# Squares of the context in a distance matrix: by ScalarE and in the bank's emptying, in place of a matmul pair, with the stage's order rewritten

## The chip, the cores and the metric

The kernel runs on 1 core of one Trainium2 chip. The metric is the device time of one execution in microseconds (us); lower is better.

## What is computed

A decoder of two layers over 64 batches of 256 tokens of width 256, with a context of 77 rows of width 256 for each batch, all in float32. Each sublayer is followed by a layer norm. What matters here is the second layer: self-attention (16 heads, rotary), and then an alignment of the context with the tokens by dynamic time warping, which begins with a matrix of Euclidean distances.

```python
def _pairwise_euclidean(a, b):
    aa = jnp.sum(a * a, axis=-1)[:, None]
    bb = jnp.sum(b * b, axis=-1)[None, :]
    ab = a @ b.T
    return jnp.sqrt(jnp.maximum(aa + bb - 2.0 * ab, 0.0))
```

Here `a` is the context (77 rows) and `b` the tokens after the layer norm (256 rows).

## The kernel before

The program has four stages, A to D, each a pass over all 64 batches, with the tokens stored to memory between them. A is self-attention of layer 0, B its cross-attention and feed-forward, C the rotary self-attention of layer 1 and the distances, D the expansion along the warping path and the last attention. Between C and D, a separate block takes the square roots and runs the warping itself.

Within a stage, a batch is a chain of steps, each named by its kind. `ORDER` gives for every engine a list of numbers, 100 x lag + place in the chain; round r of an engine's line runs, for each entry, that place of the chain for batch r - lag. So the order on each engine is written out by hand, five batches are in flight, and only semaphores tie the engines together. Adding one number of rounds to all lags of an engine changes nothing. What matters is the cyclic order of the entries and their lags relative to each other.

The steps of stage C that the text speaks of, by the names used below, with their lines on TensorE:

- "q", "k", "v": projections of the tokens, eight records each (L782 with `A_wq`, `A_wk`, `A_wv`); "oproj" is the output projection (L782 with `A_wo`). Four matmuls in float32 leave eight records, two for each.
- "max 0" to "max 3": bf16 scores from which VectorE takes row maxima (L881; VectorE L1206). "shift 0" and "shift 1" turn these maxima (L892; VectorE L1213).
- "core 0" to "core 3": scores in float32 with 32 rows of the array for each head (L814, 16 records; ScalarE's exponentials L1020, four for each core step).
- "pv 0", "pv 1": values weighted by probabilities, in 32 columns for each head (L834, 32 records). "norm" turns the result (L904).
- "xT C": turns the tokens loaded for a new batch (L792 with `Cx`); it waits for that load (SyncE, L736). "xT A3" turns the finished tokens for the distances.
- "ln": layer norm (VectorE L1270 and L1274, GpSimd L1134 to L1141). "rot": rotary on keys by VectorE (L700 to L703) and on queries by GpSimd.
- "dist": the distances. GpSimd squares the turned tokens and the turned context (L1153 to L1156, the second into `csq`, a view of the key buffer `kb`); TensorE accumulates four matmul pairs (L962); VectorE empties the bank (L1314).

The eight PSUM banks go round: each use of a bank waits until the use eight before it was emptied. SyncE has one queue in the order store of distances, load of tokens for the batch five later, fetch of the context turned, store of tokens; the load thus stands behind the wait for `dist_ready`.

The four matmuls of a distance step before:

```python
for i, (lhs, rhs) in enumerate(((ctxT[s][:, 0, :], xT[s][:, 0, :]), (ctxT[s][:, 1, :], xT[s][:, 1, :]),
                                (neg_half[:, 0:C], xsq[s][:, 0, :]), (csq[s][:, 0, :], neg_half[:]))):
    ins = pe.matmul(ck.bank(step)[0:C, 0:S], lhs, rhs, start=(i == 0), stop=(i == 3))
```

Of the kernel before, what the change touches and what calls it, by code (L numbers as in the profile page):

```python
# [33 lines left out]
S = 256  # L34
C = 77
# [139 lines left out]
def chain(phase, b):  # L175
# [10 lines left out]
    else:  # L186
# [42 lines left out]
    },  # L229
    "C": {  # L230
        "pe": (
            525, 415, 202, 307, 629, 416, 308, 203, 309, 526, 204, 417, 310, 418, 420, 312, 630, 313, 421,
            314, 423, 424, 101, 206,
        ),
        "act": (
            425, 207, 529, 317, 319, 320, 212, 322, 214, 1, 106,
        ),
        "dve": (
            204, 527, 205, 630, 313, 423, 424, 315, 102, 316, 208, 103, 209, 426, 210,
        ),  # L240
        "pool": (
            530, 323, 427, 5,
        ),
        "sp": (
            631, 100, 311, 528,
        ),
    },
    "D": {
# [45 lines left out]
def signals(step, engine):  # L294

    kind, att = step[0], step[1]
    return {
        "pe": {"core": ["scores_ready"] * 4, "pv": ["weighted"]},
        "act": {
            "q": ["q_rounded", "q_ready"] * (att in ("A1", "A2")), "qT": ["q_rounded", "q_ready"],  # L300
            "k": ["k_rounded", "k_ready"] * (att != "A3"), "kT": ["k_rounded", "k_ready"],
            "core": ["probs_ready"] * 4, "take": ["out_taken"], "xT": ["xT_ready"], "oT": ["attnT_ready"],
            "xqT": ["xqT_ready"], "gu": ["tanh_ready"], "hq": ["hid_rounded", "hq_ready"], "hT": ["hqT_ready"],
            "mix": ["exps_ready"], "v": ["v_ready"] * (att in VALUES_BY_ACT),
        },
        "dve": {
            "q": ["q_tokens"] * (att in ("A3", "A4")), "k": ["q_tokens"] * (att == "A3"), "v": ["v_ready"] * (att not in VALUES_BY_ACT),
            "rot": ["dve_step", "k_rotated"] if att == "A3" else ["norms2"],
            "max": ["max_done"] * ROW_GROUPS.get(att, 0), "shift": ["q_shifted"] * 2,
            "norm": ["dve_step", "normed"] + ["x_used"] * (att == "A1" and step[-1] == 1),  # L310
            "oproj": ["proj_taken"], "path": ["dve_step", "path_ready"], "expand": ["x4_used"],
            "down": ["down_taken"], "ln": ["dve_step", "var_ready"], "fq": ["dve_step"] * 3 + ["scales_ready"],
            "gu": ["gated", "hid_ready"], "hq": ["dve_step"] * 3 + ["scale_ready"], "dist": ["dist_ready"],
            "gate": ["logits_taken", "logits_ready"], "mix": ["dve_step"] * 5 + ["mixed"],
        },
        "pool": {
            "sq": ["squared"], "rot": ["pool_step", "rotated"] if att == "A3" else ["pool_step"] * 3 + ["rotated"],
            "xT": ["base_ready"] * (att == "B"),
            "norm": ["base_ready"] * (att in ("A3", "A4") and step[-1] == 0),
            "fq": ["pool_step", "xq_ready"], "ln": ["pool_step", "pool_step", "x_ready"], "dist": ["pool_step", "squares_ready"],  # L320
        },
        "sp": {},
    }[engine].get(kind, [])
# [61 lines left out]
def build(nc, nb, io, out):  # L385
    stack = ExitStack()
    with stack:
# [138 lines left out]
        class Tiles:  # L526


            def __init__(self, phase, where):
# [56 lines left out]
                if phase == "C":  # L586
                    self.xT, self.x = each("xT", [P, FC, S]), self.at
                    self.ctxT, self.dist = each("ctxT", [P, FC, C]), each("dist", [C, S])
                    self.csq = [t[:, 0:FC * C].rearrange("p (c n) -> p c n", c=FC) for t in self.kb_f]
                    self.xsq, self.r2, self.r3 = self.qe[0], self.res, self.ke[0]  # L590
                if phase == "D":
                    self.xT = self.atT
# [10 lines left out]
        def segment(phase, tiles, lines, counts, base, where):  # L603
# [14 lines left out]
            if phase in "CD":  # L618
                qk, qr = tiles.qk, tiles.qr
            if phase == "C":  # L620
                ctxT, csq, xsq, dist, r2, r3 = tiles.ctxT, tiles.csq, tiles.xsq, tiles.dist, tiles.r2, tiles.r3
            if phase == "D":
                path, ctx, ends, sq, nrm = tiles.path, tiles.ctx, tiles.ends, tiles.sq, tiles.nrm
                lg, ex, top, gs = tiles.lg, tiles.ex, tiles.top, tiles.gs
# [82 lines left out]
            def _(sp):  # L707
                def one(dram, b):

                    part = dram[b:b + 1] if isinstance(b, int) else dram[bass.ds(b, 1)]  # L710
                    return part.rearrange("o p n -> p o n")

                def do(ck, step):
# [23 lines left out]
                    elif kind == "fetch" and what == "A":  # L737
                        ck.wait_earlier("x_used", ("norm", "A1", b, 1))
                        sp.dma_start(x0[s][:].rearrange("p a b -> p (a b)").unsqueeze(1),
                                     one(io["x"], b)).then_inc(x_loaded[s], 16)  # L740
                    elif kind == "fetch":
                        ck.wait_earlier("dist_ready", ("dist", "A3", b))
                        sp.dma_start(ctxT[s][:].rearrange("p a b -> p (a b)").unsqueeze(1),
                                     one(io["ctxT"], b)).then_inc(ctx_loaded[s], 16)
                    elif what == "D":
                        ck.wait("dist_ready", ("dist", "A3", b))
                        sp.dma_start(one(dist_dram, b), dist[s][:].unsqueeze(1)).then_inc(dist_stored[s], 16)
                    else:
                        ck.wait("x_ready", ("ln", what, b))
                        sp.dma_start(one(x_dram[phase], b),  # L750
                                     x[s][:].rearrange("p a b -> p (a b)").unsqueeze(1)).then_inc(
                                         tokens_stored[phase][s], 16)
# [9 lines left out]
            def _(pe):  # L762
# [75 lines left out]
                def do(ck, step):  # L838
# [115 lines left out]
                    elif kind == "dist":  # L954

                        ck.wait("xT_ready", ("xT", att, b))
                        pe.wait_ge(ctx_loaded[s], 16 * (ck.turn + 1))
                        ck.wait("squares_ready", step)
                        ck.wait_bank_free(step)
                        for i, (lhs, rhs) in enumerate(((ctxT[s][:, 0, :], xT[s][:, 0, :]), (ctxT[s][:, 1, :], xT[s][:, 1, :]),  # L960
                                                        (neg_half[:, 0:C], xsq[s][:, 0, :]), (csq[s][:, 0, :], neg_half[:]))):
                            ins = pe.matmul(ck.bank(step)[0:C, 0:S], lhs, rhs, start=(i == 0), stop=(i == 3))  # L962
                        ck.filled(ins, step)
                    elif kind == "expand":
                        ck.wait("path_ready", ("path", "E", b))
# [19 lines left out]
            def _(act):  # L985
# [20 lines left out]
                def do(ck, step):  # L1006
# [59 lines left out]
                    elif kind == "hT":  # L1066
                        t = step[3]
                        ck.wait_bank_full(step)
                        ins = act.activation(hqT[s][:, t].rearrange("p a b -> p (a b)"),
                                             ck.bank(step)[:].bitcast(BF16), ACT.Copy)  # L1070
                        ck.tell(ins, "hqT_ready", step)
                    elif kind == "mix":
                        ck.wait("logits_ready", ("gate", att, b))
                        for t in range(QT):
                            for i, (low, high) in enumerate(((0, H - 1), (H - 1, H + 1))):
                                ins = act.activation(ex[s][:, t, low:high], lg[s][:, t, low:high], ACT.Exp,
                                                     bias=gs[s][:, i, t:t + 1], accum_out=gs[s][:, 2 + i, t:t + 1])
                        ck.tell(ins, "exps_ready", step)
                    else:
                        return  # L1080
# [5 lines left out]
            def _(pool):  # L1086
# [3 lines left out]
                def do(ck, step):  # L1090
# [58 lines left out]
                        ck.tell(pool.tensor_scalar(xq[s][:], xq_f[s][:], MAGIC, QMAX, ALU.subtract, ALU.min), "xq_ready", step)  # L1149
                    elif kind == "dist":  # L1150
                        ck.wait("xT_ready", ("xT", att, b))
                        pool.wait_ge(ctx_loaded[s], 16 * (ck.turn + 1))
                        pool.tensor_tensor(xsq[s][:], xT[s][:], xT[s][:], ALU.mult)  # L1153
                        link(ck, pool.tensor_tensor(csq[s][:], ctxT[s][:], ctxT[s][:], ALU.mult))
                        pool.tensor_tensor(xsq[s][:, 0, :], xsq[s][:, 0, :], xsq[s][:, 1, :], ALU.add)
                        ck.tell(pool.tensor_tensor(csq[s][:, 0, :], csq[s][:, 0, :], csq[s][:, 1, :], ALU.add),  # L1156
                                "squares_ready", step)

                walk(pool, "pool", do)
# [3 lines left out]
            def _(dve):  # L1163
# [3 lines left out]
                def do(ck, step):  # L1167
# [142 lines left out]
                        ck.wait("scale_ready", step)  # L1310
                    elif kind == "dist":
                        ck.wait_bank_full(step)
                        ck.stored(dist_stored[s])
                        ins = dve.tensor_scalar(dist[s][:], ck.bank(step)[0:C, 0:S], -2.0, 0.0, ALU.mult, ALU.max)  # L1314
                        ck.tell(ins, "dist_ready", step)
                    elif kind == "gate":
                        ck.wait_bank_full(step)
# [96 lines left out]
        with ExitStack() as where:  # L1414
# [29 lines left out]
            def _(act):  # L1444
                def root(t):
                    if t % PART == 0:
                        act.wait_ge(dist_loaded[t // PART % 2], 32 * (t // PART // 2 + 1))
                    act.activation(cost[:, t + 1, 1:W + 1], cost[:, t + 1, 1:W + 1], ACT.Sqrt).then_inc(roots_ready, 1)

                for t in range(PART):  # L1450
                    root(t)
# [129 lines left out]
```

## Time and profile before

| what | value |
|---|---|
| times of 3 runs | 5856.48, 5843.52, 5859.08 us; median 5856.48 |
| the profiled execution | 5858.39 us, its span 5856.6 us |
| TensorE busy over the span | 5289.1 us (90%) |
| VectorE busy | 4889.5 us (83%) |
| ScalarE busy | 4166.3 us (71%) |
| GpSimd busy | 2753.9 us (47%) |
| mean granted TensorE clock | 0.964 |

Stage C runs from about 2650 to 4170 us of the span. The engines' shares are means over four stages with different limits, so the rows that count are those of stage C. The 1.8 us between the execution's time and its span lie around the first and the last instruction.

### The profile page before, as it was taken

Reading aid. Unit: us, or ns where it says so; the run is one execution under the profiler, and the core shown is the slowest. Engines: PE = TensorE matmul, PEld = TensorE weight load, DVE = VectorE, ACT = ScalarE, POOL = GpSimd, SP = SyncE. Lnnn points to the kernel's source line nnn. Section 1 sums busy time; section 2 is a strip of 40 time slices with the busy share of each in tenths; the row PEclk is TensorE's granted clock in tenths of the full one; section 3 lists DMA queues with packets and bytes.
Section 4 is the critical chain, followed back from the end, with each engine's and each line's share of the span. In section 5 each row is a group of like instructions: output and inputs, shape, how many; then the busy total and the mean of one; then the engine's idle time right before and its main releaser. Section 6 shows DMA issues by size and latency. Waiting matters only on the chain. (4 is left out here: it accounts for less than half of the span.)

```text
span 5856.6 us, 138862 instructions
## 1 busy us (share of the span) xinstructions
PE 5289.1 (90%) x54914; PEld 3660.6 (63%) x54914; DVE 4889.5 (83%) x11487; ACT 4166.3 (71%) x7921; POOL 2753.9 (47%) x2766
## 2 busy tenths in 40 slices
PE   6999999969999999987999999999308999999998
PEld 4666666646666666655666666666206667666666
DVE  6888888859999999986878778778677888888887
ACT  5777777748888888875666666666326777777776
POOL 0122111125555555543545545545106777777775
PEclk9999999989999999999999999999659999999999
DMA  1111111111111111001010010010110001101000
GB/s 55 45 45 45 48 45 46 45 36 30 30 30 30 31 30 29 30 23 35 30 34 30 30 34 30 30 34 30 38 30 14 31 26 31 31 26 31 28 29 23
DMA packets 140516, 194.01 MB, mean 33 GB/s; under 512 B 26080, under 2 KB 63840, under 8 KB 139488
## 3 DMA queue, kind: packets, MB, share of 16 engines
q1 hardware_dynamic: 139872, 185.13, 10.1%
q8 instruction: 440, 7.21, 0.5%
q14 instruction: 204, 1.67, 0.1%
HBM read 112.90 MB, written 72.18 MB: 32 GB/s over the span
## 5 line engine op out<-in xcount | busy, mean ns | idle before, releaser
L1020 ACT ACTIVATE Cpr<-pj 128x512 f32<-128x512 f32 x1024 | 522.2, 614 | 426.9 <-PE pj L814 426.9
L1206 DVE TENSOR_REDUCE Amp<-pj 128x2 f32<-128x512 f32 x1024 | 629.5, 682 | 97.8 <-PE pj L881 97.8
L1206 DVE TENSOR_REDUCE Cmp<-pj 128x2 f32<-128x512 f32 x1024 | 634.4, 682 | 77.7 <-PE pj L881 77.7
L1020 ACT ACTIVATE Apr<-pj 128x512 f32<-128x512 f32 x1024 | 522.1, 613 | 172.7 <-PE pj L814 172.7
L1206 DVE TENSOR_REDUCE Dmp<-pj 128x2 f32<-128x512 f32 x1024 | 633.2, 681 | 6.1 <-PE pj L881 6.1
L1020 ACT ACTIVATE Dpr<-pj 128x512 f32<-128x512 f32 x1024 | 520.2, 610 | 101.1 <-PE pj L814 101.0
L1134 POOL TENSOR_SCALAR Ave<-Amv 128x2 f32<-128x2 f32 x64 | 14.6, 228 | 971.7 <-DVE Amv L1274 971.7
L1106 POOL TENSOR_TENSOR Dnrm<-Dnrm,power 128x32 f32<-128x32 f32 x64 | 348.8, 5449 | 122.7 <-DVE Dnrm L1184 122.7
L700 POOL TENSOR_TENSOR Cqr<-Cqk,rope_cos 128x512 f32<-128x512 f32 x64 | 81.6, 1274 | 564.0 <-DVE Cqk L1174 564.0
L1141 POOL TENSOR_SCALAR Dx<-Dres,Dmv,Drstd 128x256 f32<-128x256 f32 x256 | 312.3, 1230 | 28.9 <-POOL Drstd L1135 28.9
L1141 POOL TENSOR_SCALAR Bx<-Bres,Bmv,Brstd 128x256 f32<-128x256 f32 x256 | 311.9, 1225 | 29.6 <-POOL Brstd L1135 29.6
L814 PE MATMUL pj<-Aq,Ak 32*128 32x256 f32 x4096 | 291.5, 391 | 2.1 <-DVE Aq L1213 1.2
L814 PE MATMUL pj<-Dq,Dk 32*128 32x256 f32 x4096 | 281.9, 398 | 0.4 <-ACT Dpr L1020 0.2
L814 PE MATMUL pj<-Cq,Ck 32*128 32x256 f32 x4096 | 277.9, 395 | 1.0 <-DVE Cq L1213 0.6
L1134 POOL TENSOR_SCALAR Bve<-Bmv 128x2 f32<-128x2 f32 x128 | 29.2, 228 | 501.7 <-DVE Bmv L1274 501.7
L1020 ACT ACTIVATE Bpr<-pj 77x512 f32<-77x512 f32 x512 | 261.0, 590 | 5.1 <-PE pj L814 5.1
L968 PE MATMUL pj<-Dctx,Dkb 77*128 77x256 f32 x256 | 67.9, 388 | 210.8 <-DVE Dkb L1246 210.8
L834 PE MATMUL pj<-Dpr,Dv 128*32 128x256 f32 x4096 | 250.3, 385 | 0.2 <-ACT Dpr L1020 0.2
L834 PE MATMUL pj<-Apr,Av 128*32 128x256 f32 x4096 | 247.6, 382 | 1.3 <-ACT Apr L1020 1.1
L834 PE MATMUL pj<-Cpr,Cv 128*32 128x256 f32 x4096 | 247.6, 382 | 0.3 <-ACT Cpr L1020 0.3
L814 PEld LDWEIGHTS pj<-Cq,Ck 32*128 32x128 f32 x4096 | 193.1, 185 | 82.9 <-issue 52.4
L814 PEld LDWEIGHTS pj<-Dq,Dk 32*128 32x128 f32 x4096 | 196.5, 186 | 76.6 <-issue 67.8
(305 smaller groups left out, 15111.7 us busy)
## 6 DMA issues: line engine op xcount, KB each, us to landing
Ax0T<-in_xT SPq DMA_DIRECT2D x64, 256.0 KB, 3.0
Ax<-in_x SPq DMA_DIRECT2D x64, 256.0 KB, 3.0
x_A_scratch<-Ax SPq DMA_DIRECT2D x64, 256.0 KB, 2.1
Bx<-x_A_scratch SPq DMA_DIRECT2D x64, 256.0 KB, 2.9
x_B_scratch<-Bx SPq DMA_DIRECT2D x64, 256.0 KB, 2.0
Cx<-x_B_scratch SPq DMA_DIRECT2D x64, 256.0 KB, 3.1
x_C_scratch<-Cqr SPq DMA_DIRECT2D x64, 256.0 KB, 3.0
Dx<-x_C_scratch SPq DMA_DIRECT2D x64, 256.0 KB
```

The source lines that it names most:

```text
L700: eng.tensor_tensor(dst, src, cos, ALU.mult)
L814: ins = pe.matmul(ck.bank(step + (bank,))[0:n, at:at + S], ke[e][s][p0:p0 + 32, c, k:k + n], qe[e][s][p0:p0 + 32, c, :], start=True, stop= ...
L834: ins = pe.matmul(ck.bank(step)[r:r + VW, at:at + S], vv[s][0:n, i, h, :], probs, start=(i == 0), stop=(i == len(tiles_) - 1), skip_group_ ...
L968: ins = pe.matmul(ck.bank(step)[:, t * D:(t + 1) * D], path[s][:, t * P:(t + 1) * P], ctx[s][:], start=True, stop=True)
L1020: ck.tell(act.activation(dst, ck.bank(step + (bank,))[0:n, :], ACT.Exp, scale=HD ** -0.5), "probs_ready", step)
L1106: link(ck, pool.tensor_tensor(nrm[s][:, 1].rearrange("p t h -> p (t h)"), nrm[s][:, 0].rearrange("p t h -> p (t h)"), power[:], ALU.pow))
L1134: link(ck, pool.tensor_scalar(ve[s][:, :, 0:1], mv[s][:, :, 1:2], EPS, None, ALU.add))
L1141: ins = pool.tensor_scalar(x[s][:, t], res[s][:, t], mv[s][:, t, 0:1], rstd[s][:, t, 0:1], ALU.subtract, ALU.mult)
L1206: ins = dve.tensor_reduce(dst, src, AX.X, ALU.max, negate=True)
```

## The change

The squares of the context leave the matmul sum. SyncE fetches the context untransposed into `dist` (77 x 256) right behind the turned one. A new ScalarE step squares it in place with a sum along the row (`accum_out`) and halves the sum into `ctx_norm`. TensorE then runs three pairs, and GpSimd only squares the tokens. VectorE empties the bank by subtracting `ctx_norm` and taking the minimum with 0; the factor -2 moves into the scale of the square root. VectorE's step no longer waits for the store of five batches before, since the new fetch does.

```diff
@@ SyncE, fetch
                         sp.dma_start(ctxT[s][:].rearrange("p a b -> p (a b)").unsqueeze(1),
                                      one(io["ctxT"], b)).then_inc(ctx_loaded[s], 16)
+                        ck.stored(dist_stored[s])
+                        sp.dma_start(dist[s][:].unsqueeze(1), one(io["ctx"], b)).then_inc(ctx_loaded[s], 16)
@@ TensorE, dist
-                        pe.wait_ge(ctx_loaded[s], 16 * (ck.turn + 1))
+                        pe.wait_ge(ctx_loaded[s], 32 * (ck.turn + 1))
-                                                        (neg_half[:, 0:C], xsq[s][:, 0, :]), (csq[s][:, 0, :], neg_half[:]))):
-                            ins = pe.matmul(ck.bank(step)[0:C, 0:S], lhs, rhs, start=(i == 0), stop=(i == 3))
+                                                        (neg_half[:, 0:C], xsq[s][:, 0, :]))):
+                            ins = pe.matmul(ck.bank(step)[0:C, 0:S], lhs, rhs, start=(i == 0), stop=(i == 2))
@@ ScalarE
+                    elif kind == "dist":
+                        act.wait_ge(ctx_loaded[s], 32 * (ck.turn + 1))
+                        ck.tell(act.activation(dist[s][:], dist[s][:], ACT.Square, accum_out=ctx_norm[s][:, 0:1]), "ctx_squared", step)
+                        ck.wait("ctx_squared", step)
+                        ck.tell(act.activation(ctx_norm[s][:, 1:2], ctx_norm[s][:, 0:1], ACT.Copy, scale=0.5), "ctx_normed", step)
@@ GpSimd, dist
-                        pool.tensor_tensor(xsq[s][:], xT[s][:], xT[s][:], ALU.mult)
-                        link(ck, pool.tensor_tensor(csq[s][:], ctxT[s][:], ctxT[s][:], ALU.mult))
-                        pool.tensor_tensor(xsq[s][:, 0, :], xsq[s][:, 0, :], xsq[s][:, 1, :], ALU.add)
-                        ck.tell(pool.tensor_tensor(csq[s][:, 0, :], csq[s][:, 0, :], csq[s][:, 1, :], ALU.add),
+                        link(ck, pool.tensor_tensor(xsq[s][:], xT[s][:], xT[s][:], ALU.mult))
+                        ck.tell(pool.tensor_tensor(xsq[s][:, 0, :], xsq[s][:, 0, :], xsq[s][:, 1, :], ALU.add),
                                 "squares_ready", step)
@@ VectorE, dist
-                        ck.stored(dist_stored[s])
-                        ins = dve.tensor_scalar(dist[s][:], ck.bank(step)[0:C, 0:S], -2.0, 0.0, ALU.mult, ALU.max)
+                        ck.wait("ctx_normed", step)
+                        ins = dve.tensor_scalar(dist[s][:], ck.bank(step)[0:C, 0:S], ctx_norm[s][:, 1:2], 0.0, ALU.subtract, ALU.min)
@@ square roots, ahead of the warping
-                    act.activation(cost[:, t + 1, 1:W + 1], cost[:, t + 1, 1:W + 1], ACT.Sqrt).then_inc(roots_ready, 1)
+                    act.activation(cost[:, t + 1, 1:W + 1], cost[:, t + 1, 1:W + 1], ACT.Sqrt, scale=-2.0).then_inc(roots_ready, 1)
@@ ORDER["C"], the numbers of pool and sp (pe, act and dve are rewritten too)
-            530, 323, 427, 5,
+            523, 727, 730, 305,
-            631, 100, 311, 528,
+            200, 511, 628, 631,
```

The table for stage C is rewritten for all engines. Freed of the common number of rounds, it changes four things. On TensorE, "oproj" and "core 2" move ahead of "k", and "v" moves behind "shift 0"; all other neighbours, and all lags, stay. VectorE follows with "oproj" ahead of "k" and "v" behind "ln". GpSimd runs "dist" right behind "ln" of the same batch and ahead of the next "rot", and adds the bias for the output projection one round earlier. SyncE fetches the context one round later.

TensorE, from "max 0" to the first rows of "pv 0" in a round of stage C, before (`A_wk` is k, `A_wo` is oproj, `A_wv` is v; L814 is core 2, L892 shift 0):

```order
L881 MATMUL pj<-Ckb,Cqb_2 128x256 x8
L782 MATMUL pj<-A_wk,CxT 128x256 x4
L881 MATMUL pj<-Ckb,Cqb_2 128x256 x8
L782 MATMUL pj<-A_wo,Cqr 128x256 x4
L782 MATMUL pj<-A_wv,CxT 128x256 x4
L814 MATMUL pj<-Cq,Ck_1 128x256 x8
L892 MATMUL pj<-ident,Cmp 128x128 x2
L834 MATMUL pj<-Cpr_0,Cv 32x256 x2
```

The same place after the change, up to where "pv 0" begins (each line number is larger by 2):

```order
L883 MATMUL pj<-Ckb,Cqb_2 128x256 x8
L784 MATMUL pj<-A_wo,Cqr 128x256 x4
L816 MATMUL pj<-Cq,Ck_1 128x256 x8
L784 MATMUL pj<-A_wk,CxT 128x256 x4
L883 MATMUL pj<-Ckb,Cqb_2 128x256 x8
L836 MATMUL pj<-Cpr_0,Cv 32x256 x2
```

Two projections in a row became two with a step of 32-row scores between them, and "max 1" now stands directly ahead of "pv 0".

TensorE, from the end of "pv 0" to "max 2", before (the first L814 is core 3, the second core 0; L962 is dist):

```order
L834 MATMUL pj<-Cpr_3,Cv 32x256 x2
L814 MATMUL pj<-Cq,Ck_1 128x256 x8
L814 MATMUL pj<-Cq,Ck_2 128x256 x8
L962 MATMUL pj<-CxT,CctxT 77x256 x2
L962 MATMUL pj<-Cq,neg_half 77x256
L962 MATMUL pj<-neg_half,Ckb 77x256
L881 MATMUL pj<-Ckb,Cqb_2 128x256 x8
```

The same place after:

```order
L836 MATMUL pj<-Cpr_3,Cv 32x256 x2
L816 MATMUL pj<-Cq,Ck_1 128x256 x8
L894 MATMUL pj<-ident,Cmp 128x128 x2
L784 MATMUL pj<-A_wv,CxT 128x256 x4
L816 MATMUL pj<-Cq,Ck_2 128x256 x8
L964 MATMUL pj<-CxT,CctxT 77x256 x2
L964 MATMUL pj<-Cq,neg_half 77x256
L883 MATMUL pj<-Ckb,Cqb_2 128x256 x8
```

Core 3 and core 0 stood side by side and now have "shift 0" and "v" between them; the pair with `Ckb` (the context's squares) is gone.

ScalarE after the change, from the end of the exponentials of core 3 to the start of those of core 0:

```order
L1022 ACTIVATE Cpr_3<-pj 128x512
L1076 ACTIVATE Cdist,Cctx_norm<-Cdist 77x256
L1078 ACTIVATE Cctx_norm<-Cctx_norm 77x1
L1022 ACTIVATE Cpr_0<-pj 128x512
L1022 ACTIVATE Cpr_1<-pj 128x512
```

Before, the exponentials of core 0 followed those of core 3 with nothing between.

## Rows read from the trace of the kernel before

**Rows 1.** Windows: 200 us of stage C; PE, PEld, DVE, ACT, POOL, clock, DMA share, GB/s.

```profile
3400.00:3600.00 200.00, 196.97 (x2022) 136.74 (x2018) 159.25 (x324) 128.74 (x240) 103.66 (x117) 1.00 0.10 30
```

**Rows 2.** Waits, 2800 to 4000 us (52 rounds): total us, times, longest us.

```profile
PEld pj L792 <- DMA Cx<-x_B_scratch: 9.5, 15, 1.1
```

**Rows 3.** Timeline of TensorE in one round: start, us, line, tiles, records, idle before.

```profile
3399.99 1.99 PE L782 MATMUL pj<-A_wk,CxT 128*128 128x256 f32 x8
3401.91 0.40 PE L881 MATMUL pj<-Ckb,Cqb 32*128 32x256 bf16 x8
3402.24 1.99 PE L782 MATMUL pj<-A_wo,Cqr 128*128 128x256 f32 x8
3404.07 1.89 PE L782 MATMUL pj<-A_wv,CxT 128*128 128x256 f32 x8
3405.89 1.15 PE L814 MATMUL pj<-Cq,Ck 32*128 32x256 f32 x16
3406.97 0.44 PE L892 MATMUL pj<-ident,Cmp 128*128 128x128 f32 x2
3407.33 1.93 PE L834 MATMUL pj<-Cpr,Cv 128*32 128x256 f32 x32
3409.20 2.01 PE L814 MATMUL pj<-Cq,Ck 32*128 32x256 f32 x32
3411.14 1.09 PE L962 MATMUL pj<-CxT,CctxT 128*77 128x256 f32 x4
3412.06 0.59 PE L962 MATMUL pj<-Cq,neg_half 128*77 128x256 f32 x2
3412.49 0.59 PE L962 MATMUL pj<-neg_half,Ckb 128*77 128x256 f32 x2
3413.06 0.40 PE L881 MATMUL pj<-Ckb,Cqb 32*128 32x256 bf16 x8
3413.46 1.93 PE L834 MATMUL pj<-Cpr,Cv 128*32 128x256 f32 x32
3415.32 1.15 PE L814 MATMUL pj<-Cq,Ck 32*128 32x256 f32 x16
3416.40 1.09 PE L904 MATMUL pj<-ident,Cqk 128*128 128x128 f32 x8
3417.70 0.66 PE L792 MATMUL pj<-ident,Cx 128*128 128x128 f32 x4 [0.21 <-DMA Cx<-x_B_scratch]
3418.19 1.04 PE L792 MATMUL pj<-ident,Cqr 128*128 128x128 f32 x8
```

**Rows 4.** Timeline of VectorE in the same round.

```profile
3403.35 2.47 DVE L1206 TENSOR_REDUCE Cmp<-pj 128x2 f32<-128x512 f32 x4
...
3408.24 0.68 DVE L1196 TENSOR_TENSOR Cv<-pj,A_bv 128x512 f32<-128x512 f32 x1
...
3413.13 0.42 DVE L1314 TENSOR_SCALAR Cdist<-pj 77x256 f32<-77x256 f32 x1 [1.18 <-PE pj L962]
```

**Rows 5.** Timeline of SyncE's queue in the same round: the load of tokens.

```profile
3413.93 0.34 SPq L736 DMA_DIRECT2D Cx<-x_B_scratch  x1
```

**Rows 6.** The page, section 6: that load's median us from issue to landing.

```profile
Cx<-x_B_scratch SPq DMA_DIRECT2D x64, 256.0 KB, 3.1
```

**Rows 7.** Timeline of ScalarE in the same round: exponentials of core 3 and core 0.

```profile
3410.36 4.03 ACT L1020 ACTIVATE Cpr<-pj 128x512 f32<-128x512 f32 x8 [0.43 <-PE pj L814]
```

**Rows 8.** ScalarE in stage D: ns min/median/max, first and last start, forms.

```profile
L1036 ACT ACTIVATE Dqr<-pj,A_bv_col x128: 467/470/475, 4456.0 to 5842.2; 128x256 f32<-128x256 f32 x128
L1076 ACT ACTIVATION_READ_ACCUMULATOR Dex<-Dlg,Dgs x256: 185/191/194, 4461.9 to 5845.7; 128x1 f32 x128
```

**Rows 9.** Timeline of stage A: a GpSimd step and a VectorE step beside it.

```profile
599.62 2.58 POOL L1141 TENSOR_SCALAR Ax<-Aat,Amv,Arstd 128x256 f32<-128x256 f32 x2 [0.24 <-POOL Arstd L1135]
...
600.41 0.69 DVE L1229 TENSOR_TENSOR Aat<-Ax,Aat 128x512 f32<-128x512 f32 x1
```

**Rows 10.** A VectorE line of stage D with two inputs in SBUF (columns as rows 8).

```profile
L1337 DVE SCALAR_TENSOR_TENSOR Dgs<-Dex,Dgs x128: 146/158/1265, 4466.5 to 5846.7; 128x2 f32<-128x2 f32 x128
```

More of the change, by code:

```diff
@@ L231 @@
         "pe": (
-            525, 415, 202, 307, 629, 416, 308, 203, 309, 526, 204, 417, 310, 418, 420, 312, 630, 313, 421,
-            314, 423, 424, 101, 206,
+            321, 214, 323, 324, 1, 106, 325, 215, 2, 107, 429, 216, 108, 326, 217, 3, 109, 218, 220, 110, 4,
+            112, 430, 113,
         ),
         "act": (
-            425, 207, 529, 317, 319, 320, 212, 322, 214, 1, 106,
+            317, 319, 320, 530, 212, 322, 214, 1, 106, 325, 107, 429,
         ),
         "dve": (
-            204, 527, 205, 630, 313, 423, 424, 315, 102, 316, 208, 103, 209, 426, 210,
+            210, 427, 104, 105, 530, 213, 323, 324, 215, 2, 216, 108, 326, 3, 109,
         ),
         "pool": (
-            530, 323, 427, 5,
+            523, 727, 730, 305,
         ),
         "sp": (
-            631, 100, 311, 528,
+            200, 511, 628, 631,
         ),
@@ L303, in signals @@
             "xqT": ["xqT_ready"], "gu": ["tanh_ready"], "hq": ["hid_rounded", "hq_ready"], "hT": ["hqT_ready"],
-            "mix": ["exps_ready"], "v": ["v_ready"] * (att in VALUES_BY_ACT),
+            "dist": ["ctx_squared", "ctx_normed"], "mix": ["exps_ready"], "v": ["v_ready"] * (att in VALUES_BY_ACT),
         },
@@ L588, in __init__ @@
                     self.ctxT, self.dist = each("ctxT", [P, FC, C]), each("dist", [C, S])
-                    self.csq = [t[:, 0:FC * C].rearrange("p (c n) -> p c n", c=FC) for t in self.kb_f]
+                    self.ctx_norm = each("ctx_norm", [C, 2])
                     self.xsq, self.r2, self.r3 = self.qe[0], self.res, self.ke[0]
@@ L620, in segment @@
             if phase == "C":
-                ctxT, csq, xsq, dist, r2, r3 = tiles.ctxT, tiles.csq, tiles.xsq, tiles.dist, tiles.r2, tiles.r3
+                ctxT, ctx_norm, xsq, dist, r2, r3 = tiles.ctxT, tiles.ctx_norm, tiles.xsq, tiles.dist, tiles.r2, tiles.r3
             if phase == "D":
@@ L1151, in do @@
                         ck.wait("xT_ready", ("xT", att, b))
-                        pool.wait_ge(ctx_loaded[s], 16 * (ck.turn + 1))
-                        pool.tensor_tensor(xsq[s][:], xT[s][:], xT[s][:], ALU.mult)
-                        link(ck, pool.tensor_tensor(csq[s][:], ctxT[s][:], ctxT[s][:], ALU.mult))
-                        pool.tensor_tensor(xsq[s][:, 0, :], xsq[s][:, 0, :], xsq[s][:, 1, :], ALU.add)
-                        ck.tell(pool.tensor_tensor(csq[s][:, 0, :], csq[s][:, 0, :], csq[s][:, 1, :], ALU.add),
+                        link(ck, pool.tensor_tensor(xsq[s][:], xT[s][:], xT[s][:], ALU.mult))
+                        ck.tell(pool.tensor_tensor(xsq[s][:, 0, :], xsq[s][:, 0, :], xsq[s][:, 1, :], ALU.add),
                                 "squares_ready", step)
```

## The prediction

> **What bounds it now.** I went by stages. The page's busy shares are means over four stages, so the windows come first. In a stretch of stage C TensorE is busy 197 of 200 us at a granted clock of 1.00, which is the 2.4 GHz level; VectorE has 159, ScalarE 129, GpSimd 104 [rows 1]. TensorE bounds this stage. The waits then show where it still stands still: 15 times in 52 rounds its turning of new tokens ("xT C") stood until their load landed, 9.5 us in all and 1.1 at most [rows 2]. Last I read one round on all queues [rows 3 to 5, 7]. The distances' emptying by VectorE waited 1.18 us for TensorE [rows 4], and ScalarE's exponentials 0.43 [rows 7]: the other engines follow TensorE. A saving there counts in full, if its own cost and that load don't take it back.
>
> **The removed pair.** Between the pair with `neg_half` as weights and the pair with `Ckb` lie 0.43 us (3412.06 to 3412.49) [rows 3]. One pair less per batch is 64 x 0.43 = 27.6 us less. All of it is on the path.
>
> **The rewritten order on TensorE.** Here I price each block from its start to the start of the next, and ask what stood on both sides of it. "k", between two kinds of 32-row steps, took 1.92 (3399.99 to 3401.91). "oproj", entered from such a step and left to a projection, took 1.83, and "v", entered from a projection and left to a 32-row step, 1.82. So each border costs some 0.09 to 0.1. "Core 1", alone between "pv 1" and "norm", took 1.08, and so did "core 2". Core 3 and core 0 side by side took 1.94 (3409.20 to 3411.14), 0.22 less than two alone. "Max 1" before a projection took 0.33, "max 2" before "pv 1" 0.40 [rows 3]. In the new order:
> - core 3 and core 0 stand apart: 2.16 in place of 1.94, +0.22;
> - "oproj" now has 32-row steps on both sides: 1.92 in place of 1.83, +0.09; "k" had and has them, "v" still leaves to one and is entered from full-width work: 0 each;
> - "max 1" runs into "pv 0": 0.40 in place of 0.33, +0.07;
> - "shift 0" (0.36) is left to "v" and no longer to "pv 0": one border less, -0.09.
>
> The sum is +0.29 per round, 64 x 0.29 = 18.6 us. So the new order gives back two thirds of the pair. The trace has each of these neighbourhoods except the shift into a projection; if that were free or cost a border more, the sum would be 0.2 or 0.38, 13 or 24 us.
>
> The Trainium skill has this as a rule that speaks against the change: "TensorEngine Tiling (Array Packing)", section "Key Properties", says that changing the tiling mode drains the engine. By that rule alone, without a size, the order costs something; the rows agree, with their 0.09 to 0.22 a border.
>
> **The load behind the distances.** SyncE issues the load only after `dist_ready`. In this round it was issued at 3413.93, its median time to landing is 3.1, so it lands at 3417.03 [rows 5, 6]. TensorE could have turned it at about 3417.33: "norm" begins at 3416.40 and eight transposes take 0.93 (four take 0.49, 3417.70 to 3418.19) [rows 3]. The median margin is 0.3. What does the change do to it? Before, VectorE worked 3.71 us on "v", "ln" and "rot" (from 3408.24 until 1.18 before 3413.13) [rows 4] and was done early. Its "v" began 1.27 after "shift 0" on TensorE (3406.97) [rows 3]. After, VectorE's 1.27 + 3.71 = 4.98 after "shift 0" stand against TensorE's 0.27 ("shift 0") + 1.82 ("v") + 1.08 (core 0) + 1.49 (three pairs, from 1.92 less 0.43) + 0.03 = 4.69. So VectorE empties the distances 0.29 later than TensorE would let it, and the load loses 0.29 of its margin. The 15 rounds that wait already wait 0.29 longer, 4.4 us; of the 37 others about a quarter have less margin than that and wait half of it on average, 1 to 2 us. For 64 rounds that makes some 6 us [rows 2]. Bounds: 0 if VectorE is never late, and 64 x 0.29 = 18.6 if every round waited.
>
> **What I cost at nothing.** ScalarE's new work is a square over 77 x 256, an accumulator read and a copy of one column. The nearest rows are 0.47 for 128 x 256 from PSUM and 0.19 for the read [rows 8]; with a copy of about 0.3 (less than the 0.47) it is some 1.0 us. The cover: the eight exponentials of core 3 and core 0 began 1.16 after TensorE's start of core 3 and took 4.03 together [rows 3, 7]. Core 0 now starts 0.27 + 1.82 + 1.08 = 3.17 after core 3, while four exponentials need 2.0, so 1.16 us lie open between them. Were it to take longer, the first to wait is core 0's first bank, needed by "max 2" 2.57 after core 0 starts and free after 1.16 + 0.5: another 0.9 of room. ScalarE's wait for the fetch is a full round and more behind its landing.
>
> VectorE must end "max 1" before "shift 0": TensorE leaves 0.40 + 1.86 + 1.08 = 3.34 between their starts; VectorE needs the emptying of "k" (0.6, as the like 0.68 shape less overlap) and 2.47 for the four maxima [rows 3, 4], 3.2 with two hand-overs. That fits by 0.1; were it to miss by 0.1, 6 us come on top. GpSimd drops two of its four squares, which were off the path except for the very last batch, where they save under 1 us. "dist" on GpSimd now waits for the tokens turned in the next round ahead of "rot", whose result is needed only at that round's end. The extra fetch (77 KB a batch) is queued behind the load. VectorE's and the root's new scalars keep the shapes. Stages A, B and D don't change.
>
> **The sum.** -27.6 + 18.6 + 6 = -3.0 us. The profiled execution took 5858.4 (its span 5856.6 and 1.8 around it), which gives 5855. It lies 1.9 above the median of the runs, 5856.5, on which I set the forecast: 5853.
>
> **Rivals.**
> - *The whole pair is gained* (5829, faster). The borders cost nothing net, or the order lets something else run sooner, and the load stays hidden: -27.6. For it: TensorE is the bound at 197 of 200 us, and 37 rounds of 52 don't wait for the load. Against it: the 1.94 against 2.16 for two core steps is plain in one round. Chance 0.18.
> - *The load lands late* (slower). The new fetch and the store share the engines with the load, or VectorE's "rot" is late. The margin is 0.3, and beyond it each 0.1 costs up to 6.4 us. At 0.6 more than forecast nearly all rounds wait 0.5, +32 us, 5882; it decides from about 0.4 more. For it: the waits of up to 1.1 [rows 2] show that landings scatter by more than the margin. Against: the fetch is queued behind. Chance 0.11.
> - *GpSimd holds VectorE up* (slower). "Rot" has two inputs in SBUF and now falls beside GpSimd's layer norm (two instructions of 1.2 to 1.3). A two-element step of the same sort took 1.265 at most where 0.158 is its median [rows 10]. One such hold of 1.2 in each round would cost about 1.2 x 64 = 77 less what margin is left: 5915. Against: in stage A the same layer norm step (600 us) ran beside a VectorE step with two such inputs, which took 0.69 [rows 9], no more than a step of 128 x 512 in stage C, 0.68 [rows 4]. The Trainium skill, "GPSIMD Engine Reference", section "Key points", names this contention for VectorE instructions with two SBUF inputs. By that rule the hold would come; the trace disagrees for this pair of instructions [rows 9] and agrees for another [rows 10]. Chance 0.05.
> - My forecast, within 0.3%: 0.66.
>
> **How the numbers follow.** 0.3% is 17.6 us, about what a measurement of this kernel tells from no change. Forecast and its neighbours (order cost 13 to 24, load 0 to 18.6, a missed "shift 0" 6) span -15 to +15 and 5842 to 5868. The first rival is faster; a part of the forecast's own lower end adds to it: faster 0.20. Slower takes the second and third: 0.16. Same 0.64. The range reaches to 5831, nearly the full gain, and to 5876, where a late load begins to show.
>
> **What would show it.** In the new trace: three pairs of L964 with 0.43 less to "max 2"; core 3 and core 0 at 1.08 each, "oproj" at 1.92, "max 1" at 0.40; a round slightly under the 23.1 us of before (1200 us over 52 rounds). Waits of "xT C" for `Cx` in more rounds, 0.2 to 0.4 us longer. ScalarE's square and copy inside idle time, with no wait of VectorE's emptying on them. VectorE's emptying of the distances no longer idle before it. Wrong would be: a wait of "shift 0" for VectorE's maxima; VectorE's "rot" instructions longer beside GpSimd's layer norm; loads landing later than 3.1; or core steps apart that cost no more than together, which would give the whole pair.

## The result, and the profile after

The changed kernel took 5825.28 us in the median of 4 runs (5815.69 to 5825.86), the kernel before 5852.93 in the median of 4 beside it (5843.52 to 5859.08). The ratio is 0.995, with a 95% interval of 0.9938 to 0.9962: faster by 27.6 us. A second, later comparison (E5 below) gave 0.9954 (0.9941 to 0.9968). The forecast was 5853, at most down to 5831. So the prediction was wrong in size. The time is that of its first rival, "the whole pair is gained" (5829), but the runs below show another way to it. Two executions below, one of the ten of E2 (11572.56 us) and one of the 25 of the kernel before beside it (5965.34), ran at a lower granted clock (0.741 and 0.917, all others 0.964 to 0.967), and the ratios leave them out. The changed kernel's profiled execution took 5824.72 us.

The page of the changed kernel, sections 1 and 6: busy time, share and instructions of each engine; the token load with its median time to landing.

```profile
span 5822.9 us, 138676 instructions
PE 5262.6 (90%) x54786; PEld 3621.4 (62%) x54786; DVE 4894.9 (84%) x11487; ACT 4205.2 (72%) x8113; POOL 2746.1 (47%) x2638
...
Cx<-x_B_scratch SPq DMA_DIRECT2D x64, 256.0 KB, 3.0
```

TensorE lost 26.5 us of busy time, ScalarE gained 38.9. The 200 us of stage C that answer to [rows 1], in the windows of the changed kernel:

```profile
3400.00:3600.00 200.00, 197.23 (x2014) 135.22 (x2010) 160.88 (x326) 139.16 (x275) 99.46 (x97) 1.00 0.11 34
```

TensorE bounds the stage as before (197 of 200, at the same clock); ScalarE has 10 us more. Next, one round of TensorE, which answers to [rows 3]: the timeline, from "core 1" after "pv 1" to the next "pv 1".

```profile
3399.07 1.15 PE L816 MATMUL pj<-Cq,Ck 32*128 32x256 f32 x16
...
3406.37 0.40 PE L883 MATMUL pj<-Ckb,Cqb 32*128 32x256 bf16 x8
3406.70 1.99 PE L784 MATMUL pj<-A_wo,Cqr 128*128 128x256 f32 x8
3408.62 1.15 PE L816 MATMUL pj<-Cq,Ck 32*128 32x256 f32 x16
3409.70 1.99 PE L784 MATMUL pj<-A_wk,CxT 128*128 128x256 f32 x8
3411.62 0.40 PE L883 MATMUL pj<-Ckb,Cqb 32*128 32x256 bf16 x8
3411.95 1.93 PE L836 MATMUL pj<-Cpr,Cv 128*32 128x256 f32 x32
3413.81 1.15 PE L816 MATMUL pj<-Cq,Ck 32*128 32x256 f32 x16
3414.89 0.44 PE L894 MATMUL pj<-ident,Cmp 128*128 128x128 f32 x2
3415.16 1.89 PE L784 MATMUL pj<-A_wv,CxT 128*128 128x256 f32 x8
3416.99 1.15 PE L816 MATMUL pj<-Cq,Ck 32*128 32x256 f32 x16
3418.06 1.09 PE L964 MATMUL pj<-CxT,CctxT 128*77 128x256 f32 x4
3418.99 0.59 PE L964 MATMUL pj<-Cq,neg_half 128*77 128x256 f32 x2
3419.51 0.40 PE L883 MATMUL pj<-Ckb,Cqb 32*128 32x256 bf16 x8
3419.84 1.50 PE L836 MATMUL pj<-Cpr,Cv 128*32 128x256 f32 x24
```

From start to start: "oproj" 1.92 (forecast 1.92), core 3 (3413.81) and core 0 (3416.99) 1.08 and 1.07 (forecast 1.08 each), "shift 0" 0.27 (0.27). Two blocks differ from the forecast. "Max 1" before "pv 0" took 0.33 (3411.62 to 3411.95) and not 0.40; and "max 2" before "pv 1" now takes 0.33 as well, where it took 0.40 [rows 3]. The distances took 1.45 (3418.06 to 3419.51), 0.47 less than the 1.92 of before, though the pair is 0.43.

What TensorE's weights wait for at that place stands in the timeline of its weight loads. Before, from the distances to "pv 1":

```profile
3412.28 0.36 PEld L962 LDWEIGHTS pj<-neg_half,Ckb 128*77 128x77 f32 x2
3413.03 0.15 PEld L881 LDWEIGHTS pj<-Ckb,Cqb 32*128 32x128 bf16 x8 [0.39 <-ACT Cpr L1020]
3413.46 1.45 PEld L834 LDWEIGHTS pj<-Cpr,Cv 128*32 128x32 f32 x32 [0.28 <-ACT Cpr L1020]
```

The same in the changed kernel:

```profile
3418.77 0.36 PEld L964 LDWEIGHTS pj<-Cq,neg_half 128*77 128x77 f32 x2
3419.51 0.12 PEld L883 LDWEIGHTS pj<-Ckb,Cqb 32*128 32x128 bf16 x8 [0.37 <-ACT Cpr L1022]
3419.84 1.24 PEld L836 LDWEIGHTS pj<-Cpr,Cv 128*32 128x32 f32 x28 [0.21 <-ACT Cpr L1022]
```

The weight loads stand idle for a while here in every run; 0.37 and 0.21 are what the changed kernel and E2 below have in the mean of all rounds, 0.39 and 0.28 are more. So a wait of TensorE on ScalarE of 0.07 (and 0.02 to 0.04 ahead of "max 2") was in the trace of before, and the prediction did not use it. The releaser's name alone does not tell, since ScalarE is named in both kernels; the length does.

ScalarE in the same round, which answers to [rows 7]: timeline, with idle time before and its releaser.

```profile
3414.98 2.06 ACT L1022 ACTIVATE Cpr<-pj 128x512 f32<-128x512 f32 x4 [0.43 <-PE pj L816]
3416.90 0.42 ACT L1076 ACTIVATE Cdist<-Cdist 77x256 f32<-77x256 f32 x1
3417.20 0.21 ACT L1076 ACTIVATION_READ_ACCUMULATOR Cdist<-Cdist 77x1 f32 x1
3417.45 0.20 ACT L1078 ACTIVATE Cctx_norm<-Cctx_norm 77x1 f32<-77x1 f32 x1
3418.15 2.06 ACT L1022 ACTIVATE Cpr<-pj 128x512 f32<-128x512 f32 x4 [0.50 <-PE pj L816]
```

The eight exponentials that ran in one row are two fours now; the square, its read and the copy lie between them, 0.75 from 3416.90 to 3417.65, with 0.50 to spare. VectorE, which answers to [rows 4]:

```profile
3415.37 0.88 DVE L1217 SCALAR_TENSOR_TENSOR Cq<-pj,mask,Cq 128x256 f32<-128x256 f32 x2 [0.55 <-PE pj L894]
...
3419.18 0.69 DVE L703 TENSOR_TENSOR Cqr<-Cqr,Ck 128x512 f32<-128x512 f32 x1
3419.78 0.47 DVE L1318 TENSOR_SCALAR Cdist<-pj,Cctx_norm 77x256 f32<-77x256 f32 x1
```

VectorE waits for "shift 0" and not the reverse, though its maxima (L1210) end only 0.08 before "shift 0" begins on TensorE, near the 0.1 of the forecast. It comes to the distances without idle time, as forecast, and in the median begins emptying them 0.20 after TensorE's last pair ended, where it was 0.04 before. The waits of the changed kernel, 2800 to 4000 us (53 rounds), against [rows 2]:

```profile
PEld pj L794 <- DMA Cx<-x_B_scratch: 8.8, 17, 1.3
```

More rounds wait for the load (17 against 15), but in all no longer than before.

### The profile page after: what moved, and what is told of

Read it like the earlier page. It is cut to its first block and busy times, and to the rows that moved or that the text cites. A ratio compares the mean times of both kernels' runs of the same rounds, so it can differ in the third digit from the quotient of the medians.

```text
span 5822.9 us, 138676 instructions
## 1 busy us (share of the span) xinstructions
PE 5262.6 (90%) x54786; PEld 3621.4 (62%) x54786; DVE 4894.9 (84%) x11487; ACT 4205.2 (72%) x8113; POOL 2746.1 (47%) x2638
## 5 line engine op out<-in xcount | busy, mean ns | idle before, releaser
L1210 DVE TENSOR_REDUCE Amp<-pj 128x2 f32<-128x512 f32 x1024 | 630.0, 684 | 86.3 <-PE pj L883 86.3
L1210 DVE TENSOR_REDUCE Cmp<-pj 128x2 f32<-128x512 f32 x1024 | 634.2, 683 | 73.0 <-PE pj L883 73.0
L1210 DVE TENSOR_REDUCE Dmp<-pj 128x2 f32<-128x512 f32 x1024 | 633.8, 683 | 7.1 <-PE pj L883 7.1
L1159 POOL TENSOR_TENSOR Cq<-CxT 128x512 f32<-128x512 f32 x64 | 66.5, 1038 | 537.8 <-ACT CxT L1044 537.8
L816 PE MATMUL pj<-Cq,Ck 32*128 32x256 f32 x4096 | 295.3, 400 | 1.5 <-DVE Cq L1217 0.6
L1027 ACT ACTIVATE Cqk<-pj 128x512 f32<-128x512 f32 x128 | 76.5, 597 | 233.2 <-PE pj L836 233.2
```

The lines of the kernel that those rows point to most:

```text
L816: ins = pe.matmul(ck.bank(step + (bank,))[0:n, at:at + S], ke[e][s][p0:p0 + 32, c, k:k + n], qe[e][s][p0:p0 + 32, c, :], start=True, stop= ...
L1027: ins = act.activation(outT[s][:, 2 * octet:2 * octet + 2].rearrange("p a b -> p (a b)"), ck.bank(("pv", att, b, octet))[:], ACT.Copy)
L1159: link(ck, pool.tensor_tensor(xsq[s][:], xT[s][:], xT[s][:], ALU.mult))
L1210: ins = dve.tensor_reduce(dst, src, AX.X, ALU.max, negate=True)
```

## The experiments

Theory S (for stall): in the old order ScalarE's eight exponentials in a row hold up "max 2" and "pv 1". They began at 3410.36, one takes 0.61, and they come every 0.49 ((4.03 - 0.61) / 7). "Max 2" waits for its four banks before its first matmul, and the last of them is the one that the fifth exponential, the first of core 0, empties at 3410.36 + 4 x 0.49 + 0.61 = 3412.93; it began at 3413.06. "Pv 1" takes the bank of the sixth, free at 3413.42, and began at 3413.46 [rows 3, 7]. (In the trace these two exponentials end at 3412.92 and 3413.41.) If so, the pair alone gains nothing, because "max 2" can't come sooner; the new order alone costs its borders and gives the stall back; only both together gain. Rival B (for borders): the price of a border was misread, and pair and order each count for themselves. Rival L: the load's landings changed, because of the fetch or of GpSimd's order.

**E1: three pairs, order of before.** The changed kernel's computation, with the order of before on every engine.

```diff
         "pe": (
-            321, 214, 323, 324, 1, 106, 325, 215, 2, 107, 429, 216, 108, 326, 217, 3, 109, 218, 220, 110, 4,
-            112, 430, 113,
+            525, 415, 202, 307, 629, 416, 308, 203, 309, 526, 204, 417, 310, 418, 420, 312, 630, 313, 421,
+            314, 423, 424, 101, 206,
...
         "act": (
-            317, 319, 320, 530, 212, 322, 214, 1, 106, 325, 107, 429,
+            425, 207, 529, 530, 317, 319, 320, 212, 322, 214, 1, 106,
...
```

> The change's computation (three pairs, ScalarE's squares, GpSimd's two squares fewer) in the order of before; ScalarE's new step stands in its long idle time behind xT A3. Theory S (in the old order ScalarE's eight exponentials in a row hold max 2 and pv 1 back; the removed pair leaves TensorE only more time to wait for them): max 2 begins no earlier after core 3 than before (3.86 us), the round stays at 22.95 and the time at that of before, 5853, within 6 us. Rival P (the pair's time and some stall with it are a matter of the pair alone): the round shortens by 0.43 to 0.54 and the time is 5853 - 28 to - 34 = 5819 to 5825, that of the changed kernel.

Measured: 5849.32 (10 runs) against 5854.21 (25), ratio 0.9995 (0.9986 to 1.0005). The pair is out, and at most 8 us came of it, where its 0.43 a round would make 28. Its TensorE timeline shows where it went:

```profile
3407.36 2.01 PE L816 MATMUL pj<-Cq,Ck 32*128 32x256 f32 x32
3409.30 1.09 PE L964 MATMUL pj<-CxT,CctxT 128*77 128x256 f32 x4
3410.22 0.59 PE L964 MATMUL pj<-Cq,neg_half 128*77 128x256 f32 x2
3411.22 0.40 PE L883 MATMUL pj<-Ckb,Cqb 32*128 32x256 bf16 x8 [0.40 <-ACT Cpr L1022]
3411.62 1.93 PE L836 MATMUL pj<-Cpr,Cv 128*32 128x256 f32 x32
```

From core 3 to "max 2" it is 3.86, as before (3409.20 to 3413.06 [rows 3]). The 0.43 of the pair turned into a wait of 0.40 for ScalarE, whose eight exponentials began 1.16 after core 3, as in [rows 3, 7]. The round stayed at 22.955. All 52 rounds between 2800 and 4000 us have this wait. That is what S says; by B the round would be shorter by 0.43.

**E2: four pairs, new order.** The computation of before with the order of after (without ScalarE's new step).

```diff
         "pe": (
...
+            321, 214, 323, 324, 1, 106, 325, 215, 2, 107, 429, 216, 108, 326, 217, 3, 109, 218, 220, 110, 4,
+            112, 430, 113,
...
         "act": (
-            425, 207, 529, 317, 319, 320, 212, 322, 214, 1, 106,
+            317, 319, 320, 212, 322, 214, 1, 106, 325, 107, 429,
...
```

> The computation of before in the changed order, on all engines. Theory S: borders cost 0.21 (core 3 and core 0 apart), 0.09 (oproj) and -0.09 (shift 0), the two stalls of 0.04 and 0.07 behind dist and max 2 go: +0.10 a round, a round of 23.06 without a load wait, and 5853 + 6 = 5859. My forecast's pricing, in which 0.40 for max 2 was a border: +0.29 a round, 5871. Rival P: the order is neutral or a gain: 5853 or less.

Measured: 5857.15 (10 runs) against 5854.21, ratio 1.0005 (0.9995 to 1.0014); the round (the median spacing of VectorE's emptyings of the distances) 23.06, against 22.955 before. Its timeline, from core 0:

```profile
3407.90 1.15 PE L814 MATMUL pj<-Cq,Ck 32*128 32x256 f32 x16
3408.98 1.09 PE L962 MATMUL pj<-CxT,CctxT 128*77 128x256 f32 x4
...
3410.34 0.59 PE L962 MATMUL pj<-neg_half,Ckb 128*77 128x256 f32 x2
3410.86 0.40 PE L881 MATMUL pj<-Ckb,Cqb 32*128 32x256 bf16 x8
3411.19 1.07 PE L834 MATMUL pj<-Cpr,Cv 128*32 128x256 f32 x16
```

With all four pairs the distances take 1.88 and "max 2" 0.33: no stall. The borders cost +0.21, the stall's end gives 0.11, and the round is 0.105 longer, as the terms add up. The ratio allows 3 us less to 8 us more, which leaves no room for the 17 us (5871) of the forecast's pricing.

**E3: shorter exponentials of core 3.** The kernel before with ScalarE's exponentials of core 3 over 384 of 512 columns; the other columns of the probabilities keep old values. Order and borders stay.

```diff
+    cols = 384 if (att, step[3]) == ("A3", 3) else HALF
-    ck.tell(act.activation(dst, ck.bank(step + (bank,))[0:n, :], ACT.Exp, scale=HD ** -0.5),
+    ck.tell(act.activation(dst[:, 0:cols], ck.bank(step + (bank,))[0:n, 0:cols], ACT.Exp, scale=HD ** -0.5),
```

> The kernel before, but the four exponentials of core 3 in stage C cover 384 of 512 columns, so the other columns keep old values (part of the computation is left out). ScalarE is through with core 3 and core 0 some 0.5 us sooner. Theory S: max 2 follows dist 0.04 sooner and pv 1 follows max 2 after 0.33 in place of 0.40; the round is 22.85 in place of 22.95, the time 5853 - 7 = 5846. Rival (0.40 is what the border between max and pv costs): nothing changes on TensorE.

Measured: 5842.58 (10 runs) against 5854.21, ratio 0.9981 (0.9972 to 0.9991); round 22.845, 0.11 less. Its timeline of TensorE, from core 3:

```profile
3410.72 2.01 PE L814 MATMUL pj<-Cq,Ck 32*128 32x256 f32 x32
3412.66 1.09 PE L962 MATMUL pj<-CxT,CctxT 128*77 128x256 f32 x4
...
3414.02 0.59 PE L962 MATMUL pj<-neg_half,Ckb 128*77 128x256 f32 x2
3414.54 0.40 PE L881 MATMUL pj<-Ckb,Cqb 32*128 32x256 bf16 x8
3414.87 1.50 PE L834 MATMUL pj<-Cpr,Cv 128*32 128x256 f32 x24
```

ScalarE's eight exponentials now take 3.60 and not 4.03. Nothing of TensorE's work or order was touched, and the stall is gone: 1.88 for the distances (before 1.92), 0.33 for "max 2" (before 0.40). The 0.40 was never the price of a border. E2 and E3 both run four pairs without a stall, so their rounds give the price of the new order's borders by itself: 23.06 - 22.845 = 0.215.

**E4: the load ahead of the distances' store.** The changed kernel with SyncE's queue reordered: the load for a batch is issued most of a round (20.7 us) sooner, and it no longer stands behind `dist_ready` of the same round.

```diff
         "sp": (
-            200, 511, 628, 631,
+            628, 100, 631, 411,
```

> The changed kernel, with SyncE's load of tokens moved ahead of the store of the distances (it is issued most of a round earlier, behind the store of tokens). If the waits of xT C for its load are what is left of TensorE's idle time, they vanish: some 7 us less, 5825 - 7 = 5818, with a round of 22.63 throughout. If something else holds xT C, or the early transfer collides with another, no change.

Measured: 5823.08 (4 runs) against 5854.21, ratio 0.9947 (0.9933 to 0.9962), with a round of 22.63 throughout. No token load is waited for: the group of the turning in the lines of E4, 2800 to 4000 us (busy, mean ns, idle before), ends in 0.0,

```profile
L794 PE MATMUL pj<-ident,Cx 128*128 128x128 f32 x212 | 31.8, 273 | 0.0
```

where the changed kernel has

```profile
L794 PE MATMUL pj<-ident,Cx 128*128 128x128 f32 x212 | 33.1, 279 | 4.9 <-DMA Cx<-x_B_scratch 4.3
```

Not all of that is lost, since the other turnings (L794 with `Cqr`) stand idle for 3.8 in the changed kernel and 6.4 in E4. From the first emptying of the distances to the last, E4 took 1394.1 and the changed kernel 1397.9. E4's median was 2 us under that of the changed kernel, but the two had not run side by side.

**E5 and E6: the changed kernel and E4's side by side**, with nothing altered.

> The changed kernel once more, on the same chip as the next one, in five rounds: 5825, with a round of 22.63 and load waits of xT C of some 8 us in all.

> The changed kernel with the load of tokens ahead of the distances' store once more, beside the changed kernel in the same rounds, since 2 us between medians of four runs each told nothing. If the load waits that are gone in its profile were worth their sum, it is 7 us (0.12%) faster than the changed kernel; if they merely moved work, it is the same.

Measured, against 5856.28: E5 5832.05 (5 runs, 5821.1 to 5838.64), ratio 0.9954 (0.9941 to 0.9968); E6 5824.14 (5 runs, 5816.66 to 5830.09), ratio 0.9945 (0.9932 to 0.9957). The medians are 7.9 apart, but the intervals overlap. The group of the turning in E5's lines:

```profile
L794 PE MATMUL pj<-ident,Cx 128*128 128x128 f32 x212 | 33.8, 282 | 7.0 <-DMA Cx<-x_B_scratch 6.4
```

E6 has no such wait, and from the first emptying to the last it took 1394.4 against 1399.9 in E5. With the 3.8 of E4, the load costs the changed kernel some 4 to 6 us. E6 surely beats the kernel before (32 us), probably the changed one.

**E7 and E8: the fetch moved, GpSimd's order changed, in the kernel before.** Rival L: the changed kernel's first profile had its loads land in 3.0, the kernel before in 3.1 [rows 6]. Each was run once. E7's edit, then E8's:

```diff
         "sp": (
-            631, 100, 311, 528,
+            631, 100, 411, 528,
```

```diff
         "pool": (
-            530, 323, 427, 5,
+            523, 727, 730, 305,
```

> The kernel before with SyncE's fetch of the turned context one round later, as in the change, and nothing else. The forecast took 6 us for load waits that didn't grow: in the two kernels with the changed order the load lands after 2.85 to 2.95 us in the median, in the three with the old order after 3.1 to 3.2. If the later fetch is why, it shows here: 2.9 and load waits of about 5 us in all; if not, 3.1 and 8 to 9.

> The kernel before with GpSimd's order of the change (squares right behind the layer norm, the bias a round earlier) and nothing else. TensorE's round stays at 22.95, since GpSimd is not on its path. If GpSimd's work beside the load is what delays landings, they come after 2.9 here and not 3.1.

Measured: 5857.05 and 5850.5, both with a median landing of 3.1; the waits for the load, in the waits of E7

```profile
PEld pj L792 <- DMA Cx<-x_B_scratch: 7.5, 12, 1.1
```

and of E8

```profile
PEld pj L792 <- DMA Cx<-x_B_scratch: 7.6, 14, 1.1
```

against 9.5 and 15 rounds [rows 2]. Neither shortens a landing, and neither shortens the round (22.955 in both, the same as before). E5, the changed kernel again, landed at 3.1 as well, so its first 3.0 may be a matter of the execution; E2, with the whole new order, landed at 2.9 in its one profile, and why stays open. As the cause of the gain rival L falls: the changed kernel gains as much in E5, where the landing is that of before.

## Why the prediction was wrong

- **The pair** (-0.43 a batch) was sized right, 3412.06 to 3412.49 [rows 3]. But "all of it is on the path" holds only in the new order. In the old one its round gains nothing, since "max 2" follows ScalarE there (E1). The forecast took both from one round of the old order. It did work out when core 0's first bank comes free for "max 2" in the new order (0.9 of room) but not in the old one, where the same sum gives 3412.93, with "max 2" due at 3413.02 (1.88 after 3411.14) and no room for the hand-over.
- **The rewritten order on TensorE** is the step that failed. Of its four borders three came out as priced: core 3 and core 0 apart +0.21 (forecast +0.22), "oproj" +0.09, "shift 0" -0.09. The fourth did not: "max 1" before "pv 0" +0.07 was read from "max 2" before "pv 1", whose 0.40 was 0.33 of work and 0.07 of waiting for ScalarE (E2 and E3). And the same wait, 0.07 plus 0.04 ahead of "max 2", ends in the new order, a gain that the sum lacked. Together 0.07 + 0.11 = 0.18 a round, 64 x 0.18 = 11.5 us: the order costs 0.105 a round, 6.7 us, and not 0.29 and 18.6.
- "The other engines follow TensorE" was the reading behind it. The timeline of TensorE names no idle time for ScalarE in that round; the stall stood in the weight loads as 0.28 where 0.21 is the mean without it (E2).
- The Trainium skill's rule that a change of tiling mode drains the engine ("TensorEngine Tiling (Array Packing)", section "Key Properties") agrees with E2 and E3: at equal work and without a stall, the order with more borders has a round longer by 0.215. That it is a draining no run shows. For the bf16 scores before "pv" no run shows a cost: they take 0.33 there as before a projection.
- **The load behind the distances** (+6) was mis-sized. VectorE does come to the distances without idle time, as forecast, but later than TensorE would let it by some 0.16 (0.20 less 0.04) and not 0.29. More rounds wait (17 and 23, against 11 to 15 in the five profiles of the old order), and TensorE's weight loads waited 8.8 and 12.1 us in all, against 7.1 to 9.7. In the spacing of VectorE's emptyings little of that is left. Over the first 59 of the 63 spacings, the time beyond 59 times the median is 3.4 and 5.7 us in the changed kernel's two profiles, 5.2 in the kernel before and 3.1 to 5.5 in the other four: about nothing within this scatter.
- **What was costed at nothing** held: ScalarE's step took 0.75 (forecast 1.0) with 0.50 to spare; "shift 0" was not delayed; VectorE's four steps of "rot" took 0.68, 0.42, 0.42 and 0.69 in the median against 0.66, 0.42, 0.42 and 0.69 before, so GpSimd did not hold them. The rule of "GPSIMD Engine Reference", section "Key points" (Trainium skill), on which that rival stood, showed on VectorE here by 0.03 at most.
- **The first rival** (5829) came out in its number. Of its reasons the first did not hold, since the borders cost 0.215 a round; the second, that the order lets something else run sooner, holds for the 0.11 of the stall. Of the 27.6 the terms below find only some 21 to 24, so the match is in part luck.
- **Smaller slips of the forecast's sums**, which decide nothing: the load's 5.4 to 6.4 us in 52 rounds are 6.6 to 7.9 in 64; the upper end of the neighbours is +21 and not +15 with the missed "shift 0"; a late load's +32 gives 5885 and not 5882. The round of before is 22.955, and not 23.1.

The sum with the measured terms, for 64 rounds: pair -27.6, borders 64 x 0.215 = +13.8, stall 64 x -0.11 = -7.0, load about 0, in all -20.8. A round without a load wait fell from 22.955 to 22.63, 0.325, which is 20.8 in 64: the three terms add up to it. By the same terms three pairs in the old order without a stall would have a round of 22.845 - 0.43 = 22.415; this is an estimate, and no run has tried it. The whole stage shows it as well; VectorE's emptying of the distances by source, before and after (x64: ns min/median/max, first and last start):

```profile
L1314 DVE TENSOR_SCALAR Cdist<-pj x64: 420/421/422, 2745.4 to 4168.9; 77x256 f32<-77x256 f32 x64
```

```profile
L1318 DVE TENSOR_SCALAR Cdist<-pj,Cctx_norm x64: 472/474/480, 2738.4 to 4136.3; 77x256 f32<-77x256 f32 x64
```

That is 1423.5 and 1397.9 from first to last. E1, E7 and E8, whose round is that of before, took 1420.9, 1421.9 and 1418.6, E5 1399.9. So the change is worth some 19 to 26 us in this stage. Part of it lies in the last rounds, in which the pipeline empties: the last four spacings were 64.0 in all before and in E7, 59.1 after and in E5. Four steady rounds account for 1.3 of these 4.9 us, but E1, E2, E3 and E8 had 61.0 to 61.5. So some 1 to 4 us come on top of the 20.8, and which part of the change brings them was not taken apart. From the last emptying to the end all ten profiles took 1685.4 to 1687.7. The 7 us by which stage C began sooner in the changed kernel's profile (2738.4) are not the change's, since stages A and B are the same program and E5 began at 2751.1. The measured -27.6 has an interval of 22 to 36 (from the ratio), the second comparison one of 19 to 35; the sum of some -21 to -24 lies inside the second and at the lower edge of the first. Whether the few microseconds between them are chance or a further effect stays open.

## What to carry to other kernels

Before you price a neighbour of a step from a trace, look whether another engine gates it: work out when each PSUM bank it writes comes free, and compare the idle time of its weight loads with that of a like step elsewhere in the round. A gain on the bounding engine is worth what the next constraint leaves of it, so a removed step and a reordering can each be worth nothing and both together a third of a microsecond a round; test them apart and together. And look at a load that is queued behind a late result: where its buffer is free, it can be issued sooner, which in E4 and E6 ended its waits for some 4 to 6 us.

## What the runs showed of the hardware that was not expected

GpSimd's root of two columns in the layer norm took 1.25 in the median where it now falls beside VectorE's "rot", and 0.75 before; by source, before and after:

```profile
L1135 POOL TENSOR_TENSOR Crstd<-Cve,power x64: 723/747/751, 2720.5 to 4157.2; 128x2 f32<-128x2 f32 x64
```

```profile
L1142 POOL TENSOR_TENSOR Crstd<-Cve,power x64: 725/1246/1248, 2714.9 to 4126.5; 128x2 f32<-128x2 f32 x64
```

So where the two met, GpSimd was the one that lost, half a microsecond; VectorE's steps beside it lost 0.03 at most in the median. E2 shows the same (1.24), E8, with GpSimd's order alone, does not (0.75). In stage D it is the other way round: of the 128 steps of [rows 10] 61 took 0.58 to 1.27 and not 0.158, and each of them ran while a GpSimd step with two inputs in SBUF (L1115, 1.27), begun before it, was still running, and ended with that step. What they contended for was not tried. VectorE's emptying of the distances takes 474 ns with the operand from a tile (`ctx_norm`) where it took 421 with constants; the two operations changed with it (subtract and minimum in place of multiply and maximum).
